# Layer 1's cross-attention in a decoder kernel: from two rounds over all queries to four quarters, with two key tiles in TensorE's row halves and the next quarter's maxima beside the units

## The chip, the cores and the metric

The kernel runs on one core of a Trainium2 chip. The metric is the device time of one execution in microseconds, lower is better. Of the engines, PE is TensorE, DVE is VectorE, ACT is ScalarE, POOL is GpSimd and SP is SyncE; each runs its own instruction stream and waits on semaphores. PE's clock has two levels, 1.2 and 2.4 GHz; the profile gives the granted share of the higher one.

## The reference

The kernel computes a two-layer decoder on x (1,024 tokens of 128 features) with a context of 6,404 rows of 96 features. What matters here is layer 1's cross-attention. Keys and values come from the context by two quantized projections to `image_embeds`, and the queries are `fused` (1,024 × 128):

```python
for Wa, ba in ((W_att0, b_att0), (W_att1, b_att1)):
    kv = bitnet_linear(image_embeds, Wa, ba)          # 6404 x 64
    k = jnp.concatenate([kv, kv], axis=-1)
    scores = jnp.einsum('bse,bpe->bsp', fused, k) * inv_sqrt_e
    attn = jax.nn.softmax(scores, axis=-1)
    fused = fused + 0.1 * jnp.einsum('bsp,bpe->bse', attn, k)
```

It is two rounds of softmax attention, the second on the first one's result. As the keys are the same 64 features twice, the kernel adds the two halves of `fused` once and works with 64 features. Both uses of `kv`, as keys and as values, go through the same attention.

## The kernel before

**Tiles.** The 6,404 keys are 51 tiles of 128 (KT, the last with 4 keys); 26 units (NU) hold two tiles each, the last one tile. Scores stand in PSUM with keys on partitions and queries along the row. Queries are split into halves of 512 (HALF).

**A round** (r = 0, 1) has a head and a loop.

The head: PE multiplies `fused` by DUP (L2044), ACT copies the queries to f16 (L947, QH) and DVE makes the low part (L1499, QL). Then `max_alone` finds, for each query, the maximum over all keys. It uses max(a, b) = (a + b)/2 + |a − b|/2: PE makes half-differences (bank 0 or 2 and the one behind) and half-sums (bank 4 or 6 and the one behind) from LK16 (L1692), ACT writes the magnitudes (L717, MC), and DVE adds and reduces both in one instruction (L1078). ALONE1 lists its steps: 3 chunks of 1,024 times 8 query tiles, and a rest of 130 columns for all tiles, so 24 large evictions and 8 small ones on DVE. `shifts` (L1099) and `diagonals` (L1105) turn the maxima into diagonal matrices, and `seeds` (L1714) puts −maximum into the four score banks.

The loop over 26 units: `scores` (L1729) accumulates three products of high and low f16 parts per tile (KL·QH, KH·QL, KH·QH); in each, two matmuls with 64 rows, one per query half, use the two row halves of PE and write banks 2b and 2b+1. ACT takes exp of a tile for all 1,024 queries (L738) into PR, two units deep. PE multiplies it with the values of the tile in fp32 (L1744), behind the scores of the next unit; the two query halves go to the two column halves. DVE adds each tile to ACC (L1128). At the end, `denominators` (L1756) sums ACC over partitions, DVE takes reciprocals (L1134) in two halves and normalizes (L1143), adds the bias (L1517) and updates `fused` in XT (L1521); `fused_upd` lets PE go on with round 1's head.

**Work beside.** In round 0's loop the keys and values of round 1 are prepared: 14 SIDES (sums and differences for the maxima, L1906 and L1907, evicted by ACT at L861 and L864) in bank 5, and 20 NEXT_KV: 7 groups of values (L1898, L847) and 13 of keys (L1892 and L1893, high part by ACT at L841, low part by DVE at L1439) in banks 6 and 7. Round 1's loop has nothing beside it.

**Layer 0** has a cross-attention of the same form. There the maxima of the next pair of heads run beside the loop: `max_steps` on PE (L1776), `magnitude` on ACT (L758), `maximum` on DVE (L1078), 512 columns a step, with bank 6 for the one half and bank 7 for the other. A step waits for two counters, and DVE's loop sets where its part stands:

```python
e.wait_ge(S("x_cp"), micro_base(p) + m)        # max_steps, PE
e.wait_ge(S("mx"), micro_base(p) + m - 1)

add_up(*before, 0)                              # loop, DVE
maximum(p, first)
add_up(*before, 1)
maximum(p, last)
```

**Order.** Each engine's order is written out by hand in the loops over units; nothing is planned at run time. The next stage (f1, f2 and the low-rank tail) waits for the maximum of the updated `fused` (L1524 to L1526), which POOL reduces over partitions (L608). SP loads that stage's weights (L493, L494) once the last unit's buffers are free.

Of the kernel before, what the change touches and what calls it, by code (L numbers as in the profile page):

```python
# [69 lines left out]
ALONE1 = full_then_rest(NDC - 1, lambda t: (t % 2,), 6)  # L70
# [16 lines left out]
def unit_no(hf, i):  # L87
    return hf * NU + i
# [104 lines left out]
def kv_bank(x):  # L193
    return 6 + NEXT_KV.index(x) % 2


def kv_freed(r, x):

    if x[0] == "dk":
        return "lk_lo", r * NKP + x[1] + 1  # L200
    return "vt_ev", r * NVT + x[1] + 1

# [35 lines left out]
def build_decoder(nc, x_tm, x_fm, ctx_fm, small, pair_w, moe_w, sh_gu, sh_d, bit_w, lr_a, lr_b, out):  # L238
    with ExitStack() as ctx:
# [33 lines left out]
        TMPB = KN[1][:, 4 * T:4 * T + 2 * LAG].bitcast(F32)  # L273
# [123 lines left out]
        AVG = sb("AVG", [P, 4])  # L397
# [21 lines left out]
        OO = W_[1]  # L419
# [8 lines left out]
        def attention_operands(hf):  # L428

            if hf < 2 * PAIRS:  # L430
                p, u = divmod(hf, 2)
                q = [slice(u * HALF, (u + 1) * HALF)] * 2
                kh, kl, qh, ql = KH, KL, QH[p % 2], QL[p % 2]
                shift = [DIAG[:, h, 4 * u:4 * u + 4, :].rearrange("p a b -> p (a b)") for h in range(2)]

                def v(r, j, h):
                    return V[0:r, j, h * HD:(h + 1) * HD]
            else:
                n = hf - 2 * PAIRS
                q = [slice(h * HALF, (h + 1) * HALF) for h in range(2)]  # L440
                kh, kl, qh, ql = LKH[n], LKL[n], QH[1], QL[1]
                shift = [DIAG[:, h, 0:4, :].rearrange("p a b -> p (a b)") for h in range(2)]

                def v(r, j, h):
                    return V2[n][0:r, j, :]
            return kh, kl, qh, ql, q, shift, v
# [5 lines left out]
        def _(q):  # L452
# [38 lines left out]
            q.wait_ge(S("pv"), unit_no(2 * PAIRS + 1, NU - 1) + 1)  # L491
            q.wait_ge(S("acc"), (2 * PAIRS + 2) * KT)
# [11 lines left out]
        def _(e):  # L504
# [87 lines left out]
            e.sem_inc(S("dup"), 1)  # L592
            e.wait_ge(S("ln_x"), 2 * NT)
# [12 lines left out]
            for i in range(3, 6):  # L606
                e.wait_ge(S("ax"), i + 1)
# [8 lines left out]
        def _(e):  # L616
# [327 lines left out]
            for r in range(2):  # L944
# [1228 lines left out]
```

## Time and profile before

| | |
|---|---|
| runs | 1724.82, 1729.21 (median), 1729.83 us |
| profiled execution | 1728.0 us, span 1726.3 us, mean granted clock 0.916 |
| PE busy | 1516.9 us (88%) |
| DVE busy | 1291.2 us (75%) |
| ACT busy | 1118.8 us (65%) |
| POOL busy | 433.0 us (25%) |
| chain that ended last | PE 64%, DVE 14%, issue 13%, POOL 5%, ACT 3% |

Busy shares are averages over stages with different limits, so they only say where to look first. The chain is followed back from the last instruction, at each step to what released it; "issue" is time in which an engine waited for nothing that the profile shows. A matmul's recorded duration holds its way through the array, so where matmuls follow each other, the distance from start to start is what each costs.

### The profile page before, as it was taken

The numbers are of one execution on the slowest core, as the hardware profiler recorded it, in microseconds if no ns is written. First come the engines' busy times: TensorE is split into PE (matmuls) and PEld (weight loads), VectorE is DVE, ScalarE is ACT, GpSimd is POOL, SyncE is SP. The second block draws the span as 40 slices with busy tenths as digits, with TensorE's granted clock in tenths as the row PEclk, the third lists the DMA queues.
The fourth block names the chain that finished last, engine by engine and source line by source line (L and its number), as shares of the span: only waits on it lengthen the run. The fifth ranks groups of instructions, "written<-read, shape, count | busy, mean of one in ns | idle before, by whom it ended". The sixth has DMA issues, their size and how long they took to land.

```text
span 1726.3 us, 26028 instructions
## 1 busy us (share of the span) xinstructions
PE 1516.9 (88%) x8864; PEld 542.1 (31%) x8864; DVE 1291.2 (75%) x2214; ACT 1118.8 (65%) x1496; POOL 433.0 (25%) x413
## 2 busy tenths in 40 slices
PE   3878889999999999999999997899996869978963
PEld 2412223333333333333332333343333612311312
DVE  4798688777888778887789898766665676778775
ACT  3687667776777767867767686655553466746633
POOL 5401333343443434433400010344441000000000
PEclk7966889999999999999999998999998958986986
DMA  4000000000000000000010000111100000000000
GB/s 127 7 0 6 1 1 2 1 1 1 8 1 1 1 1 3 1 1 10 20 32 1 1 1 22 32 41 46 41 27 0 1 0 1 1 1 1 1 13 12
DMA packets 12556, 20.26 MB, mean 12 GB/s; under 512 B 1670, under 2 KB 11254, under 8 KB 12342
## 3 DMA queue, kind: packets, MB, share of 16 engines
q1 hardware_dynamic: 12438, 18.76, 3.9%
q8 instruction: 66, 1.08, 0.3%
q14 instruction: 52, 0.43, 0.1%
HBM read 18.23 MB, written 0.52 MB: 11 GB/s over the span
## 4 chain that ended last, share of the span: by engine, by line
PE 64%; DVE 14%; issue 13%; POOL 5%; ACT 3%; DMA 1%; POOLq 0%; SPq 0%; ACTq 0%; DVEq 0%
PE PS L1744 26%; PE PS L1729 18%; PE PS L1776 4%; POOL WRK L599 4%; DVE KNB L1078 4%; PE PS L1692 3%; PE PS L1619 2%; PE PS L1611 2%; DVE WRK L1128 1%; DMA KNB<-in_ctx_fm_dram 1%; DVE QS L1134 1%; PE PS L2020 1%; PE PS L2005 1%; ACT KNB L758 1%; ACT WRK L738 1%
## 5 line engine op out<-in xcount | busy, mean ns | idle before, releaser
L1128 DVE TENSOR_TENSOR WRK<-WRK 128x768 f32<-128x768 f32 (+1 forms) x500 | 550.4, 1101 | 57.2 <-ACT WRK L738 45.1
L738 ACT ACTIVATE WRK<-PS 128x1024 f32<-128x1024 f32 (+1 forms) x510 | 500.0, 1022 | 104.9 <-PE PS L1729 90.7
L1744 PE MATMUL PS<-WRK,V 128*64 128x512 f32 (+1 forms) x2040 | 498.0, 608 | 0.0
L1078 DVE CUSTOM_DVE_ANT_0 KNB<-PS,KNB 128x512 f16<-128x512 f32 (+2 forms) x464 | 331.4, 731 | 150.9 <-PE PS L1776 139.0
L572 POOL TENSOR_TENSOR WRK<-WRK 128x256 f32<-128x256 f32 x300 | 277.8, 926 | 411.7 <-ACT WRK L738 394.5
L758 ACT ACTIVATE KNB<-PS 128x512 f16<-128x512 f32 (+2 forms) x306 | 181.1, 592 | 108.3 <-PE PS L1776 108.2
L1916 PE MATMUL PS<-WRK,KNB 128*128 128x512 f16 x828 | 198.1, 384 | 11.0 <-POOL WRK L599 4.3
L1744 PEld LDWEIGHTS PS<-WRK,V 128*64 128x64 f32 (+1 forms) x2040 | 124.3, 136 | 247.8 <-issue 199.1
L1729 PE MATMUL PS<-Q,KB 64*128 64x512 f16 (+1 forms) x1428 | 192.7, 379 | 0.5 <-ACT WRK L738 0.4
L1729 PE MATMUL PS<-KNB,KB 64*128 64x512 f16 (+1 forms) x1224 | 156.3, 377 | 0.0
L599 POOL TENSOR_TENSOR WRK<-KB,WRK 128x1024 f16<-128x1024 f32 x46 | 98.6, 2143 | 133.9 <-ACT WRK L884 133.9
L1916 PEld LDWEIGHTS PS<-WRK,KNB 128*128 128x128 f16 x828 | 77.3, 98 | 123.1 <-issue 23.1
L717 ACT ACTIVATE KNB<-PS 128x1024 f16<-128x1024 f32 x96 | 97.9, 1023 | 27.3 <-DVE MXP L1078 15.5
L1300 DVE TENSOR_TENSOR KA<-PS,KB 128x1024 f32<-128x1024 f32 x46 | 56.3, 1224 | 72.6 <-ACT KB L871 72.6
L884 ACT ACTIVATE WRK<-KB 128x1024 f16<-128x1024 f32 x46 | 48.6, 1057 | 90.3 <-DVE KB L1306 87.0
L1729 PEld LDWEIGHTS PS<-Q,KB 64*128 64x128 f16 (+1 forms) x1428 | 65.5, 94 | 128.8 <-ACT WRK L738 44.1
L1776 PE MATMUL PS<-KNB,Q 64*128 64x512 f16 (+1 forms) x448 | 80.0, 360 | 27.5 <-DVE MXP L1078 17.0
L608 POOL PARTITION_ALL_REDUCE AM<-AX x3 | 1.1, 371 | 380.6 <-DVE AX L1526 295.6
L1729 PEld LDWEIGHTS PS<-KNB,KB 64*128 64x128 f16 (+1 forms) x1224 | 59.9, 94 | 63.5 <-issue 12.0
L1692 PE MATMUL PS<-CTX,Q 64*128 64x512 f16 x192 | 50.8, 606 | 15.0 <-DVE MXP L1078 7.0
L1729 PE MATMUL PS<-Q,KA 64*128 64x512 f16 (+1 forms) x408 | 62.0, 383 | 0.0
L666 ACT ACTIVATE V<-PS 128x512 f32<-128x512 f32 (+1 forms) x52 | 30.1, 580 | 48.6 <-PE PS L1619 48.0
(333 smaller groups left out, 1501.0 us busy)
## 6 DMA issues: line engine op xcount, KB each, us to landing
V<-in_moe_w_dram SPq DMA_DIRECT2D x44, 192.0 KB, 2.4
KNB<-in_ctx_fm_dram SPq DMA_DIRECT2D x1, 2401.5 KB, 18.5
CTX<-in_ctx_fm_dram SPq DMA_DIRECT2D x6, 384.0 KB, 4.4
BW<-in_bit_w_dram SPq DMA_DIRECT2D x1, 960.0 KB, 6.2
PWK<-in_pair_w_dram SPq DMA_DIRECT2D x4, 192.0 KB, 2.6
SM<-in_small_dram SPq DMA_DIRECT2D x1, 716.5 KB, 4.6
XT<-in_x_fm_dram SPq DMA_DIRECT2D x1, 512.0 KB, 5.5
X<-in_x_tm_dram SPq DMA_DIRECT2D x1, 512.0 KB, 7.4
```

What stands on the lines that cost most here:

```text
L572: e.tensor_tensor(total, total, part, ALU.add).then_inc(S("acc_pool"), 1)
L599: e.tensor_tensor(H_LO[hslot], MH[hslot % 2], H_HI[hslot], ALU.subtract).then_inc(S("h_lo"), 1)
L717: e.activation(MC[:, m % 2, :], bank(b, b + 2), ACT.Abs).then_inc(S("x_cp"), 1)
L738: e.activation(PR[0:r, u % 2, b, :], bank(2 * b, 2 * b + 2, slice(0, r)), ACT.Exp).then_inc(S("exp"), 1)
L758: e.activation(MC[:, m % 2, 0:w], PS[:, 6, 0:w], ACT.Abs).then_inc(S("x_cp"), 1)
L1078: return e.tensor_tensor_reduce(diffs, sums, diffs, 0.5, NEG, ALU.add, ALU.max, accum_out=out)
L1128: e.tensor_tensor(total, total, part, ALU.add).then_inc(S("acc"), 1)
L1692: ins = e.matmul(o, queries[rows, tiles[0] * P:(tiles[0] + 1) * P], keys[rows, at:at + HALF], start=True, stop=True)
L1729: ins = e.matmul(PS[0:r, 2 * b + h, :], keys[rows, j * P:j * P + r], queries[rows, q[h]], start=False, stop=(k == 2), skip_group_check=True)
L1744: ins = e.matmul(PS[h * HD:(h + 1) * HD, 4, :], v(r, j, h), PR[0:r, unit_no(hf, i) % 2, b, h * HALF:(h + 1) * HALF], start=(j == 0), stop= ...
L1776: ins = e.matmul(PS[:, b, k * w:(k + 1) * w], QH[(p + 1) % 2][rows, t * P:(t + 1) * P], K16[rows, off + a:off + a + w], start=True, stop=True)
L1916: ins = e.matmul(bank(b + h), w_[:, part, :], rows[:, h * HALF:(h + 1) * HALF], start=start and i == 0, stop=stop and i == 2, skip_group_c ...
```

## The change

Instead of two rounds over 1,024 queries there are four quarters n: round n // 2, query half n % 2. A quarter has 26 units of two key tiles and 512 queries. In `scores1` the two row halves of PE hold the two tiles of a unit; in `values1` the two column halves sum even and odd tiles apart, and a matmul with DUP (`fold`) adds the halves at the end. Only quarter 0's maxima run alone, for half of the queries; those of quarter n + 1 run in quarter n (STEPS1, 26 steps of 512 columns or a rest), from unit 0 in quarter 0 and from unit 8 in quarters 1 and 2. The exponentials have four buffers (PR1). Keys and values of round 1 are spread over quarter 0 (14 sides, 7 values, 5 keys) and quarter 1 (8 keys), all in bank 5. The queries of quarters 2 and 3 are projected in unit 6 of quarters 1 and 2, after `fold` has updated their half of `fused` in unit 4. POOL adds the bias to XT ahead of time. The distance of the key differences is 512 instead of 256, and the quantization of the queries (L1491) loses its clamps.

Constants and lists:

```diff
-ALONE1 = full_then_rest(NDC - 1, lambda t: (t % 2,), 6)
+ALONE1 = [(d, [t], t % 2) for d in range(NDC - 1) for t in range(NT // 2)] + [(NDC - 1, [0, 1, 2, 3], 0)]
...
+STEPS1 = [(c, [t], t % 2) for c in range(NFULL) for t in range(NT // 2)] + [(NFULL, [0, 1, 2], 0), (NFULL, [3], 1)]
+NM1 = len(STEPS1)
...
+def steps1(n, i):
...
+    first, last = (0 if n == 0 else 8), NU - 2
+    if n + 1 == QUARTERS or not first <= i <= last:
+        return []
+    k = last - first + 1
+    return list(range((i - first) * (NM1 + 1) // k, (i - first + 1) * (NM1 + 1) // k))
...
+def items1_of(n):
+    at = {i: [] for i in range(NU)}
+    if n == 0:
+        for k, x in enumerate(SIDES):
+            at[k].append(("side", x))
+        for k, x in enumerate(NEXT_KV[:NU - len(SIDES)]):
+            at[len(SIDES) + k].append(x)
+    else:
+        at[1].append(("den", n - 1))
+        at[2].append(("den2", n - 1))
+        at[4].append(("fold", n - 1))
+        if n < 3:
+            at[6].append(("query", n + 1))
+        if n == 1:
+            for k, x in enumerate(NEXT_KV[NU - len(SIDES):]):
+                at[0 if k == 0 else 7 + k].append(x)
+    return at
```

POOL:

```diff
+                if i == 4:
+                    for k, (r, part) in enumerate(((0, slice(0, T)), (1, slice(0, HALF)), (1, slice(HALF, T)))):
+                        e.wait_ge(S("f2_ps"), k + 1)
+                        e.tensor_scalar(XT[:, part], XT[:, part], BT1[:, r:r + 1], None, ALU.add).then_inc(S("pre_b"), 1)
```

ACT:

```diff
+            def exp1(n, i):
...
+                e.wait_ge(S("sc"), BEFORE_SC + t + 1)
+                if t >= len(PR1):
+                    e.wait_ge(S("pv"), BEFORE_PV + t - len(PR1) + 1)
+                    e.wait_ge(S("acc"), BEFORE_SC + t - len(PR1) + 1)
...
+                    ins = e.activation(PR1[t % len(PR1)], bank(b, b + 2), ACT.Exp)
...
+            def magnitude1(n, steps):
...
+                    e.wait_ge(S("x_ps"), k + 1)
+                    e.wait_ge(S("mx"), k - 1)
+                    e.activation(MC[:, (k - BASE1) % 2, 0:w], PS[:, 6, 0:w], ACT.Abs).then_inc(S("x_cp"), 1)
...
+            for n in range(QUARTERS):
                 for i in range(NU):
...
+                    magnitude1(n, steps1(n, i)[0:1])
+                    exp1(n, i)
+                    magnitude1(n, steps1(n, i)[1:])
+                    if i == 0 and n:
+                        copy_out1(n - 1)
+                    for x in ITEMS1[n][i]:
+                        bank5_1(x)
```

DVE:

```diff
-            quantize(XQ, bank(0, 2), XF, 3).then_inc(S("quant"), 1)
+            link(e.tensor_scalar(XF, bank(0, 2), AI[:, 3:4], MAGIC, ALU.mult, ALU.add))
+            e.tensor_scalar(XQ, XF, MAGIC, None, ALU.subtract).then_inc(S("quant"), 1)
...
+            def maximum1(n, steps):
...
+                for s in steps:
+                    m = s - 1
...
+                    e.wait_ge(S("y_ps"), k + 1)
+                    e.wait_ge(S("x_cp"), k + 1)
+                    for z, t in enumerate(tiles):
+                        ins = half_max(MXP[:, 4 * ((n + 1) % 2) + t, c:c + 1], PS[:, 7, z * w:(z + 1) * w],
+                                       MC[:, (k - BASE1) % 2, z * w:(z + 1) * w])
+                    ins.then_inc(S("mx"), 1)
...
+            def fold(n):
...
+                e.scalar_tensor_tensor(XT[:, part], bank(5), 0.1, XT[:, part], ALU.mult,
+                                       ALU.add).then_inc(S("fused_upd"), 1)
...
+            for quarter in range(QUARTERS):
                 for i in range(NU):
...
+                    if i:
+                        add_up1(quarter, i - 1)
+                    elif quarter:
+                        add_up1(quarter - 1, NU - 1)
+                    maximum1(quarter, steps1(quarter, i))
+                    for x in ITEMS1[quarter][i]:
+                        bank5_1(x)
+                    if quarter + 1 < QUARTERS and i == NU - 1:
+                        shifts1(quarter + 1)
```

PE:

```diff
+            def scores1(n, i):
...
+                if t >= 2:
+                    e.wait_ge(S("exp"), BEFORE_SC + t - 1)
+                if i < 2:
+                    e.wait_ge(S("diag"), 2 * PAIRS + n + 1)
+                    for g in range(2):
+                        e.matmul(bank(b + g), ones16[:, :], DIAG[:, u, 0:4, :].rearrange("p a b -> p (a b)"), start=True,
+                                 stop=False, skip_group_check=True)
+                for k, (keys, queries) in enumerate(((LKL[r], QH[1]), (LKH[r], QL[1]), (LKH[r], QH[1]))):
+                    for g in tiles_of(i):
+                        j = 2 * i + g
+                        w = rows_of(j)
+                        rows = slice(g * HD, (g + 1) * HD)
+                        ins = e.matmul(PS[0:w, b + g, :], keys[rows, j * P:j * P + w], queries[rows, q], start=False,
+                                       stop=(k == 2), skip_group_check=True)
...
+            def values1(n, i):
...
+                e.wait_ge(S("exp"), BEFORE_SC + t + 1)
...
+                for g in tiles_of(i):
+                    j = 2 * i + g
+                    w = rows_of(j)
+                    ins = e.matmul(PS[g * HD:(g + 1) * HD, 4, :], V2[n // 2][0:w, j, :],
+                                   PR1[t % len(PR1)][0:w, g * HALF:(g + 1) * HALF], start=(i == 0),
+                                   stop=(j >= KT - 2), skip_group_check=True)
...
+            def denominators1(n):
+
+                e.wait_ge(S("acc"), BEFORE_SC + (n + 1) * NU)
+                for k in range(2):
+                    for g in range(2):
+                        ins = e.matmul(PS[g * HD:(g + 1) * HD, 5, :], ones[:, 0:HD],
+                                       ACC[:, n % 2, k * HALF:(k + 1) * HALF], start=(k == 0), stop=(k == 1),
...
+            def fold(n):
+
+                e.wait_ge(S("on"), 2 * PAIRS + n + 1)
+                e.matmul(bank(5), DUP, ON[:, n % 2 * HALF:(n % 2 + 1) * HALF], start=True,
...
+            def max_steps1(n, steps):
...
+                    if m < NM1:
+                        e.wait_ge(S("x_cp"), base + m)
+                    e.wait_ge(S("mx"), base + m - 1)
+                    if m < NM1:
+                        max_half1(n, m, 0, 6, "x_ps")
+                    if m:
+                        max_half1(n, m - 1, NH, 7, "y_ps")
...
                 for i in range(NU):
...
+                    max_steps1(n + 1, steps1(n, i)[0:1])
+                    scores1(n, i)
+                    max_steps1(n + 1, steps1(n, i)[1:])
+                    for x in ITEMS1[n][i]:
+                        bank5_1(x)
                     if i:
...
+                        values1(n, i - 1)
+                    elif n:
+                        values1(n - 1, NU - 1)
+            values1(QUARTERS - 1, NU - 1)
+            denominators1(QUARTERS - 1)
+            fold(QUARTERS - 1)
```

## Rows read from the trace of the kernel before

**Rows 1.** Busy time by stage: start:end, length, busy time by engine, PEclk, DMA share, GB/s

```profile
1394.27:1429.64 35.37, 26.95 (x112) 5.21 (x112) 31.80 (x67) 27.00 (x28) 0.00 (x0) 0.50 0.00 1
1429.64:1531.12 101.48, 101.48 (x621) 30.65 (x621) 71.84 (x66) 70.71 (x87) 0.00 (x0) 0.98 0.00 1
1531.12:1582.60 51.48, 32.84 (x126) 6.90 (x124) 40.32 (x77) 27.34 (x29) 0.00 (x0) 0.58 0.00 1
1582.60:1667.55 84.95, 84.46 (x511) 25.18 (x510) 61.97 (x51) 49.55 (x51) 0.00 (x0) 0.99 0.00 1
```

**Rows 2.** Timeline, head of round 0: start, us, engine, line, operation [idle before <-releaser]

```profile
1384.14 0.69 DVE L1230 TENSOR_SCALAR WRK<-WRK 128x1024 f32<-128x1024 f32 x1
...
1396.49 1.23 DVE L1078 CUSTOM_DVE_ANT_0 KNB<-PS,KNB 128x1024 f16<-128x1024 f32 x1 [2.36 <-ACT KNB L717]
...
1428.29 1.29 DVE L1105 TENSOR_TENSOR DIAG<-ident,NEGM 128x512 f16<-128x512 f16 x2
1429.64 1.89 PE L1714 MATMUL PS<-DIAG,ones 128*128 128x512 f16 x4 [2.91 <-DVE DIAG L1105]
```

**Rows 3.** Timeline, one unit of round 1

```profile
1657.41 0.39 PE L1729 MATMUL PS<-Q,KB 64*128 64x512 f16 x2
...
1658.27 1.94 ACT L738 ACTIVATE WRK<-PS 128x1024 f32<-128x1024 f32 x2 [1.33 <-PE PS L1729]
...
1658.81 1.94 PE L1744 MATMUL PS<-WRK,V 128*64 128x512 f32 x8
...
1659.33 2.56 DVE L1128 TENSOR_TENSOR WRK<-WRK 128x1024 f32<-128x1024 f32 x2 [0.71 <-ACT WRK L738]
...
1660.67 0.39 PE L1729 MATMUL PS<-Q,KB 64*128 64x512 f16 x2
```

**Rows 4.** Timeline: one tile's scores (round 1's end), one tile's values (layer 0)

```profile
1663.94 0.38 PE L1729 MATMUL PS<-Q,KB 64*4 64x512 f16 x2
...
1664.68 0.65 PE L1744 MATMUL PS<-WRK,V 128*64 128x512 f32 x2
...
1043.54 1.03 PE L1744 MATMUL PS<-WRK,V 128*64 128x512 f32 x4
...
1044.50 1.47 PE L1729 MATMUL PS<-Q,KB 64*128 64x512 f16 x12
```

**Rows 5.** Timeline of layer 0: a maxima pair, then two pairs in a one-tile unit

```profile
483.91 0.39 PE L1776 MATMUL PS<-KNB 64*128 64x512 f16 x2
484.13 1.46 PE L1729 MATMUL PS<-Q,KB 64*128 64x512 f16 x12
...
277.65 0.39 PE L1776 MATMUL PS<-KNB,Q 64*128 64x512 f16 x2
...
278.11 0.69 DVE L1078 CUSTOM_DVE_ANT_0 KNB<-PS,KNB 128x512 f16<-128x512 f32 x1 [0.44 <-PE PS L1776]
...
278.95 0.39 PE L1776 MATMUL PS<-KNB,Q 64*128 64x512 f16 x2 [0.17 <-DVE MXP L1078]
```

**Rows 6.** Timeline of layer 0: PE held by a late maximum on DVE

```profile
226.61 0.68 DVE L1078 CUSTOM_DVE_ANT_0 KNB<-PS,KNB 128x512 f16<-128x512 f32 x1
...
227.22 0.95 DVE L1128 TENSOR_TENSOR WRK<-WRK 128x768 f32<-128x768 f32 x1
...
227.45 0.61 PE L1776 MATMUL PS<-KNB,Q 64*128 64x512 f16 x2 [7.29 <-DVE MXP L1078]
```

**Rows 7.** Groups by form, 1428.6 to 1534.4: count | busy us, mean ns | idle before

```profile
L738 ACT ACTIVATE WRK<-PS 128x1024 f32<-128x1024 f32 x50 | 48.6, 1024 | 8.6 <-PE PS L1729 7.8
...
L1439 DVE SCALAR_TENSOR_TENSOR KB<-PS,WS,KA 128x512 f16<-128x512 f32 x11 | 8.3, 751 | 1.4 <-ACT KA L841 1.3
...
L841 ACT ACTIVATE KA<-PS,WS 128x512 f16<-128x512 f32 x11 | 7.6, 687 | 11.9 <-PE PS L1893 11.9
```

**Rows 8.** Timeline of the tail

```profile
1672.81 1.97 DVE L1517 TENSOR_SCALAR WRK<-ON,SM 64x512 f32<-64x512 f32 x4
...
1677.92 0.35 POOL L608 PARTITION_ALL_REDUCE AM<-AX  x1 [295.58 <-DVE AX L1526]
```

More of the change, by code:

```diff
@@ L592, in _ @@
             e.sem_inc(S("dup"), 1)
+            for r in range(2):
+                link(e.tensor_scalar(BT1[:, r:r + 1], sm(f"b_att{r}"), 0.1, None, ALU.mult))
             e.wait_ge(S("ln_x"), 2 * NT)
@@ new lines, in bank5_1 @@
+            def bank5_1(x):
+                kind, a = x
+                if kind == "side":
+                    sums_and_differences(1, *a, 5)
+                elif kind == "query":
+                    part = slice(a % 2 * HALF, (a % 2 + 1) * HALF)
+                    e.wait_ge(S("f2_ps"), a)
+                    if a == 2:
+                        e.wait_ge(S("sc"), BEFORE_SC + NU)
+                    else:
+                        e.wait_ge(S("sc"), BEFORE_SC + 2 * NU)
+                    e.activation(QH[1][:, part], bank(5), ACT.Copy, scale=D ** -0.5).then_inc(S("f2"), 1)
+                elif kind in ("values", "dk"):
+                    kv(1, x)
@@ new lines, in max_half1 @@
+            def max_half1(n, m, off, b, name):
+                c, tiles, g = STEPS1[m]
+                r, u = divmod(n, 2)
+                a, w = MCH[c]
+                rows = slice(g * HD, (g + 1) * HD)
+                for k, t in enumerate(tiles):
+                    ins = e.matmul(PS[:, b, k * w:(k + 1) * w], QH[1][rows, (4 * u + t) * P:(4 * u + t + 1) * P],
+                                   LK16[r][rows, off + a:off + a + w], start=True, stop=True)
+                ins.then_inc(S(name), 1)
@@ new lines, in _, with bank5_1 @@
+            order1 = {x: k for k, x in enumerate(ORDER1)}
+            def bank5_1(x):
+                kind, a = x
+                if kind == "den2":
+                    return
+                if order1[x]:
+                    name, count = freed1(ORDER1[order1[x] - 1])
+                    e.wait_ge(S(name), count)
+                if kind == "side":
+                    sums_and_differences(1, *a, 5, 0)
+                elif kind == "den":
+                    denominators1(a)
+                elif kind == "fold":
+                    fold(a)
+                elif kind == "query":
+                    e.wait_ge(S("fused_upd"), a - 1)
+                    e.matmul(bank(5), DUP, XT[:, a % 2 * HALF:(a % 2 + 1) * HALF], start=True,
+                             stop=True).then_inc(S("f2_ps"), 1)
+                else:
+                    kv(1, x)
```

299 lines of the change are left out of this document (178 added, 121 removed).

## The prediction

> **What bounds the kernel now.** I read the page first: PE is busy for 88% of the span and holds 64% of the chain that ended last, so PE is the suspect. An average doesn't tell what one stage is worth, so I cut layer 1's cross-attention into its stages [rows 1]. Both unit loops are PE's: 101.48 and 84.95 us in which PE is busy throughout at a granted clock of 0.98 and 0.99. The head of a round is not: in the 35.37 us before the first loop DVE is busy for 31.80, and PE's clock is at 0.50, its lower level (1.2 GHz). Between the loops 51.48 us go by with the same head and the end of round 0. So there are some 87 us in which PE could do other work, and that is what the change is after.
>
> In a unit of round 1 [rows 3] the score matmuls start at 1657.41, exp at 1658.27 (0.86 later), the value matmuls at 1658.81, and the next unit at 1660.67: 3.26 us for two key tiles and all 1,024 queries. The two row halves already work at the same time: two matmuls together are recorded as 0.39 long, and twelve start within 1.40 us.
>
> **The change, part by part.** The sum is made against the profiled execution's 1728.0 us, which is 1.2 below the median of the runs.
>
> *Head.* Between DVE's first large eviction and the diagonals [rows 2] lie 24 large and 8 small evictions, 31.8 us. The new list has 12 and 4: −15.9. One diagonal of two: −0.65. Two shift matmuls of four ahead of the first scores: −0.9. The quantization drops one pass of 0.69. Together −18.1.
>
> *Packing.* Two key tiles in the row halves instead of two query halves saves no PE time: six matmuls per tile and 1,024 queries before, six per two tiles and 512 queries after. It makes the units smaller: 104 instead of 52. With one tile's scores between, values start 0.74 after scores (three passes of 0.22 and 0.09 of change-over), and one tile's values take 0.96 until the next scores [rows 4]: 1.70 a unit, where half of 3.26 is 1.63. So 104 units cost 7 us more than 52 did. The Trainium skill (TensorEngine Tiling (Array Packing), Key Properties) states that a change of tiling mode drains TensorE, and scores and values use different modes; the trace agrees in direction, 0.07 a unit. Without it the sum would be 7 lower.
>
> *Other PE work.* A pair of maxima matmuls, sums and differences in opposite row halves, holds PE for 0.22 [rows 5]; 27 steps a quarter make 5.9 in each of quarters 0 to 2. Round 0's loop is longer than round 1's by 16.5; less 1.9 for its four shifts at low clock, 14.6 is the price of its 34 side, value and key items: 0.43 each. Denominators take two fp32 passes instead of one, 1.85 (twice 0.93, half of the 1.86 of [rows 3]); a fold and a query projection 0.95 each, at the same price; shifts for two units 1.0.
>
> PE alone would need: quarter 0: 44.2 + 5.9 + 26 × 0.43 + 0.5 − 0.96 (no values in its first unit) = 60.8; quarter 1: 44.2 + 5.9 + 8 × 0.43 + 1.0 + 1.85 + 1.9 = 58.4; quarter 2: 54.9; quarter 3: 48.0. Sum 222.1, with 1.0 for the last values 223.1.
>
> *The new wait.* Maxima have one bank for sums (6) and one for differences (7). In quarters 1 and 2 they may run in units 8 to 24 alone: 27 steps in 17 units, so 10 units hold two. There PE issues step a, scores, step b, then the value matmuls; step b waits until DVE has evicted the differences that step a issued. Nothing on PE passes that wait: values, and the next unit's scores, stand behind it. In layer 0 this round trip shows: a at 277.65, eviction at 278.11, b at 278.95 with "<-DVE MXP" [rows 5]: 1.30, where PE alone would need 0.87. And there DVE was free. When DVE is late, PE's wait is as long as that takes: 7.29 us once [rows 6], from an eviction's start to PE 0.84.
>
> Here DVE is late in each such unit, since it first adds up the unit before: 1.23 [rows 3], of which the next instruction overlaps 0.05. From the start of that addition, b comes 1.18 + 0.84 = 2.02 later; the differences that b issues reach DVE 0.46 later [rows 5], their eviction takes 0.62 (226.61 to 227.22) [rows 6], and the next addition can start: 3.10 a unit, after another such unit. After a unit with one step the addition itself waits for exp: 0.22 (pair) + 0.86 + 1.02 + 0.04 = 2.14 [rows 3, 5, 7] after that unit's start, which is 0.22 into the next; b at 2.24, then 0.22 + 0.09 + 0.96 [rows 4]: 3.51. PE alone would need 1.70 + 0.44 = 2.14. A unit with one step stays at 1.92: its wait ends 1.81 after its start. So a pair of steps costs 0.96 or 1.37 of pure waiting.
>
> Quarter 2 has 7 of the one kind and 3 of the other: 12.5. Quarter 1 has 6 without key items (4 × 1.37 + 2 × 0.96 = 7.4, and 0.7 where the two kinds meet), and 4 with one: there ACT evicts the key item behind the second magnitude, DVE takes another 0.75 behind ACT's 0.69 [rows 7], and the next addition waits for that. The same count gives 4.8 after one single and 4.4 after another double, where PE needs 2.6: 3 × 2.1 + 1.8 = 8.1.
>
> Smaller waits: the fold behind 3.4 us of reciprocals, 0.6 in each of quarters 1 to 3; the shifts at the ends of quarters 1 and 2, 0.6 each; in quarter 0 two double units 3.0, bank 5's key items handed on through DVE 2.0, the low clock of its first units 1.3, its end, where the shifts stand behind a key item on DVE, 2.0.
>
> Quarters: 60.8 + 8.3 = 69.1; 58.4 + 17.4 = 75.8; 54.9 + 13.7 = 68.6; 48.0 + 0.6 = 48.6. With the last values 263. Before, from the first scores to the denominators, 236.1 (1431.5 to 1667.55) [rows 1]. So +26.9: the 51.5 between the loops are gone, and the loops themselves take 78 more.
>
> *Tail.* Denominators +0.9. From 1672.81 to the all-reduce at 1677.92 [rows 8], 5.1, is replaced by a fold at low clock (two passes of 0.85 and 0.25 of hand-over), an addition over half the width (0.7 and a gap of 0.2), half a maximum (0.6) and 0.25: 3.85. Net −0.35.
>
> *At nothing.* POOL's three additions of the bias: POOL is idle in all four stages [rows 1], and each is wanted tens of us later. ACT needs 2.2 us of a 2.4 us unit in quarter 0; if it doesn't fit, up to 0.2 in 14 units, 3 us, which the range holds. SP's last loads stand behind the same event as before, and their consumers behind the fold. No DMA is added.
>
> Sum: −18.1 + 26.9 − 0.35 = +8.4 on 1728.0; on the median, **1738**.
>
> **Rivals.**
> *Faster: the second step costs its round trip alone.* If DVE has its addition behind it when step a issues, each of the 20 double units waits 0.43 [rows 5] instead of 0.96 to 2.1: 8.6 instead of 28.0, so 11.0 below before: 1718. For it: in layer 0 two steps a slot cost PE nothing but their 0.22 when scores of two tiles lay between. Against: there an eviction stands ahead of the addition on DVE, here the addition stands ahead in the code, and it can't start before exp is done. It decides where the mean wait of a double unit is under 1.0 us. If nothing waited at all, 223 us of PE time would give 1698.
> *Slower: PE's clock falls.* In the double units PE streams for some 60 to 70% of the time. In the head its clock is 0.50 with evictions as the pace [rows 1]; in both loops, with PE busy throughout, 0.98 or more. No row shows a stage between these. At the lower level each unit takes 1.7 longer; for half of the 34 units with maxima +29: 1766. The Trainium skill (TensorE: Matmul & The Clock Gate, Part 1) states that this clock is gated by how busy PE has been; the trace agrees, with 0.50 in the head.
> *It doesn't do what it says: maxima don't run beside.* If the first step of a quarter waited for the query projection of its unit 6, steps would bunch up. The projection is done about 3.4 us after unit 6 starts, two units take longer than that; I give it nothing.
>
> **How the numbers follow.** 0.65 for the forecast, 0.20 for the round trip alone, 0.05 for no waits, 0.10 for the clock. The forecast's own range is 1727 to 1751: a third of its 40 us of waits either way. The range that holds 8 in 10, 1712 to 1752, adds the first rival; 1698 and 1766 stay out. A measurement of this kernel tells 0.3%, 5 us, from no change. Forecast: 0.42 slower, 0.18 within, 0.05 faster; round trip: 0.16 faster, 0.04 within; no waits: faster; clock: slower. Together 0.26 faster, 0.22 same, 0.52 slower.
>
> **What would show it.** Right: the head some 16 us shorter; quarters of about 69, 76, 68 and 49 us; in quarters 1 and 2, units 8 to 24, PE idle before the second maxima pair with DVE's maxima as releaser, about 1 to 2 us each, and DVE's addition right before that eviction; units of 1.70 in quarter 3. Wrong: quarters 1 and 2 at 60 or less, idle time under 0.5 before those pairs (first rival); a granted clock under 0.9 in quarter 1 or 2 (second); units of quarter 3 far from 1.70 (packing mis-sized).

## The result, and the profile after

The kernel after takes 1742.36 us in the median of its runs (1741.44 to 1742.88) against 1727.03 for the kernel before, measured beside it (four runs, three of them those of the table ahead, whose median is 1729.21): a ratio of 1.0087, 95% interval 1.0073 to 1.0101. That is 15 us slower. The profiled execution took 1741.99, its span 1740.3.

The first view is the busy time in windows, one for each quarter from its first shift matmul to the next quarter's (the last one to the denominators), then four windows around the end of quarter 0. The columns are those of [rows 1].

```profile
1412.51:1485.26 72.75, 67.94 (x398) 18.04 (x401) 50.72 (x90) 56.66 (x79) 0.00 (x0) 0.92 0.00 1
1485.26:1562.66 77.40, 63.59 (x341) 16.17 (x344) 57.43 (x98) 47.13 (x62) 1.56 (x1) 0.98 0.00 1
1562.66:1630.76 68.10, 58.13 (x329) 15.06 (x328) 52.04 (x90) 42.46 (x54) 1.56 (x1) 1.00 0.00 1
1630.76:1681.74 50.98, 50.70 (x273) 11.87 (x271) 36.47 (x34) 26.76 (x27) 0.00 (x0) 1.00 0.00 1
...
1469.00:1477.00 8.00, 5.73 (x38) 1.73 (x34) 7.43 (x11) 5.61 (x9) 0.00 (x0) 1.00 0.00 0
1478.47:1485.26 6.79, 5.90 (x13) 0.96 (x14) 3.56 (x6) 1.96 (x3) 0.00 (x0) 0.50 0.00 0
1485.26:1488.71 3.45, 3.45 (x11) 0.67 (x12) 0.45 (x1) 1.00 (x1) 0.00 (x0) 0.50 0.03 7
1488.71:1493.00 4.29, 3.53 (x16) 0.90 (x18) 1.35 (x2) 2.23 (x4) 0.00 (x0) 1.00 0.00 0
```

Where [rows 1] had both loops filled by PE, PE now stands for 4.8, 13.8 and 10.0 us of quarters 0 to 2; only the last quarter, which has no maxima beside it, is PE's throughout. Around the end of quarter 0, from 1478.47 to 1488.71, the granted clock is 0.50, the lower level (1.2 GHz).

The waits of PE from 1409 to 1690 us, by line and releaser (total us, times, longest), name the cause in their first row: L2283 is the matmul of a maxima step. The second row is the folds; its longest wait, 4.2, is that of the tail.

```profile
PE PS L2283 <- DVE MXP L1193: 25.5, 24, 1.8
PE PS L2273 <- DVE ON L1258: 5.0, 4, 4.2
PE PS L2235 <- DVE DIAG L1617: 1.7, 2, 1.1
```

The timeline of the kernel after (start, us, engine, line, operation, idle time before and its releaser), in four pieces: the head's first maxima matmul and the first shift matmul behind it; the end of quarter 0; a unit of quarter 2 with two steps; a unit of quarter 3, and the tail.

```profile
1393.62 1.86 PE L1871 MATMUL PS<-CTX,Q 64*128 64x512 f16 x6 [2.54 <-DVE Q L1607]
...
1412.51 1.04 PE L2235 MATMUL PS<-DIAG,ones 128*128 128x512 f16 x2 [1.11 <-DVE DIAG L1617]
...
1477.79 0.23 PE L2283 MATMUL PS<-CTX,Q 64*128 64x130 f16 x1 [1.78 <-DVE MXP L1193]
...
1478.49 1.97 PE L2255 MATMUL PS<-WRK,V 128*64 128x512 f32 x4
...
1480.39 0.58 PE L2242 MATMUL PS<-Q,KB 64*4 64x512 f16 x1
...
1489.62 0.60 PE L2235 MATMUL PS<-DIAG,ones 128*128 128x512 f16 x2
...
1589.41 0.39 PE L2283 MATMUL PS<-CTX,Q 64*128 64x512 f16 x2
...
1589.57 1.23 DVE L1632 TENSOR_TENSOR WRK<-WRK 128x1024 f32<-128x1024 f32 x1 [0.58 <-ACT WRK L1020]
...
1590.71 0.68 DVE L1193 CUSTOM_DVE_ANT_0 KNB<-PS,KNB 128x512 f16<-128x512 f32 x1
...
1591.55 0.39 PE L2283 MATMUL PS<-CTX,Q 64*128 64x512 f16 x2 [1.10 <-DVE MXP L1193]
...
1591.87 1.08 PE L2255 MATMUL PS<-WRK,V 128*64 128x512 f32 x4
...
1592.88 0.39 PE L2283 MATMUL PS<-CTX,Q 64*128 64x512 f16 x2
...
1647.27 0.39 PE L2242 MATMUL PS<-Q,KB 64*128 64x512 f16 x2
...
1648.02 1.08 PE L2255 MATMUL PS<-WRK,V 128*64 128x512 f32 x4
1649.03 0.39 PE L2242 MATMUL PS<-Q,KB 64*128 64x512 f16 x2
...
1681.74 1.94 PE L2265 MATMUL PS<-WRK,ones 128*64 128x512 f32 x8
...
1687.88 2.08 PE L2273 MATMUL PS<-ON,DUP 128*128 128x512 f32 x2 [4.20 <-DVE ON L1258]
...
1691.73 0.38 POOL L670 PARTITION_ALL_REDUCE AM<-AX  x1 [110.80 <-DVE AX L1705]
```

The head, from its first maxima matmul at 1393.62 to the first shift matmul at 1412.51, is 18.9 us long, where [rows 1] had 35.37. In the double unit the first step is issued at 1589.41. Its half-sums lie ready, but DVE adds up the preceding unit's weights until 1590.71, then evicts them, and the second step starts at 1591.55; the values follow it. The unit takes 3.47 us, of which PE stands for 1.10. A plain unit of quarter 3 takes 1.76 us, 0.75 from scores to values and 1.01 from values to the next scores. From the denominators at 1681.74 to the all-reduce are 9.99 us, 10.37 before (1667.55 to 1677.92 in [rows 1, 8]).

So the head and the tail are shorter, and still the all-reduce comes at 1691.73 instead of 1677.92 [rows 8], 13.8 us later. The time went into the quarters.

### The profile page after: what moved, and what is told of

The parts are those of the page before. It is cut to its first block, busy times and chain, and to the rows that moved or that the text cites. A ratio compares the mean times of both kernels' runs of the same rounds, so it can differ in the third digit from the quotient of the medians.

```text
span 1740.3 us, 26359 instructions
## 1 busy us (share of the span) xinstructions
PE 1528.2 (88%) x8887; PEld 538.7 (31%) x8900; DVE 1293.7 (74%) x2290; ACT 1131.2 (65%) x1537; POOL 442.5 (25%) x418
## 4 chain that ended last, share of the span: by engine, by line
PE 62%; DVE 14%; issue 14%; POOL 5%; ACT 4%; DMA 1%; POOLq 0%; DVEq 0%; SPq 0%; ACTq 0%
PE PS L1922 20%; PE PS L1908 13%; PE PS L2255 5%; PE PS L1954 4%; POOL WRK L657 4%; DVE KNB L1193 4%; PE PS L2242 3%; PE PS L1798 2%; PE PS L1790 2%; PE PS L1871 2%; PE PS L2283 1%; DVE WRK L1243 1%; DVE QS L1249 1%; DMA KNB<-in_ctx_fm_dram 1%; PE PS L2196 1%
## 5 line engine op out<-in xcount | busy, mean ns | idle before, releaser
L800 ACT ACTIVATE WRK<-PS 128x1024 f32<-128x1024 f32 (+1 forms) x408 | 400.9, 1022 | 58.2 <-PE PS L1908 44.5
L1243 DVE TENSOR_TENSOR WRK<-WRK 128x768 f32<-128x768 f32 (+3 forms) x400 | 427.2, 1068 | 14.2 <-ACT WRK L800 7.6
L1922 PE MATMUL PS<-WRK,V 128*64 128x512 f32 (+1 forms) x1632 | 398.9, 609 | 0.0
L1922 PEld LDWEIGHTS PS<-WRK,V 128*64 128x64 f32 (+1 forms) x1632 | 99.7, 136 | 197.0 <-issue 161.9
L1908 PE MATMUL PS<-Q,KB 64*128 64x512 f16 (+1 forms) x1224 | 152.6, 377 | 0.0
L1632 DVE TENSOR_TENSOR WRK<-WRK 128x1024 f32<-128x1024 f32 (+1 forms) x100 | 119.9, 1199 | 29.5 <-ACT WRK L1020 28.4
L1020 ACT ACTIVATE WRK<-PS 128x1024 f32<-128x1024 f32 x100 | 102.4, 1024 | 53.6 <-PE PS L2242 50.2
L2255 PE MATMUL PS<-WRK,V 128*64 128x512 f32 (+1 forms) x408 | 113.8, 626 | 0.3 <-issue 0.3
L1410 DVE TENSOR_TENSOR KA<-PS,KB 128x1024 f32<-128x1024 f32 x46 | 56.3, 1225 | 72.7 <-ACT KB L934 72.7
L1908 PEld LDWEIGHTS PS<-Q,KB 64*128 64x128 f16 (+1 forms) x1224 | 55.6, 94 | 89.1 <-ACT WRK L800 21.1
L779 ACT ACTIVATE KNB<-PS 128x1024 f16<-128x1024 f32 x60 | 61.2, 1024 | 17.4 <-DVE MXP L1193 9.7
L1044 ACT ACTIVATE KNB<-PS 128x512 f16<-128x512 f32 (+1 forms) x78 | 45.3, 581 | 32.5 <-PE PS L2283 31.9
```

The lines of the kernel that those rows point to most:

```text
L800: e.activation(PR[0:r, u % 2, b, :], bank(2 * b, 2 * b + 2, slice(0, r)), ACT.Exp).then_inc(S("exp"), 1)
L1243: e.tensor_tensor(total, total, part, ALU.add).then_inc(S("acc"), 1)
L1632: e.tensor_tensor(total, total, part, ALU.add).then_inc(S("acc"), 1)
L1908: ins = e.matmul(PS[0:r, 2 * b + h, :], keys[rows, j * P:j * P + r], queries[rows, :], start=False, stop=(k == 2), skip_group_check=True)
L1922: ins = e.matmul(PS[h * HD:(h + 1) * HD, 4, :], V[0:r, j, h * HD:(h + 1) * HD], PR[0:r, unit_no(hf, i) % 2, b, h * HALF:(h + 1) * HALF], s ...
L2255: ins = e.matmul(PS[g * HD:(g + 1) * HD, 4, :], V2[n // 2][0:w, j, :], PR1[t % len(PR1)][0:w, g * HALF:(g + 1) * HALF], start=(i == 0), st ...
```

## The experiments

Theory W says that PE stands because the reduction of a unit's first step waits on DVE behind the addition, and the second step, the values and the next unit wait for it. Theory M says that the halved units cost, since PE goes from scores (64 rows) to values (128 rows) and back twice as often. Theory C says that the low clock at the end of quarter 0 carries the loss.

The code ahead of the first shift matmul is the same in all these kernels, yet in their profiles that matmul starts anywhere between 1409.29 and 1417.26 us. So I compare one stretch by the traces, from that matmul to the all-reduce of the tail, and give the time beside it. Quarters 0 to 2 run from their first shift matmul to the next quarter's.

One part of this stretch comes from no edit. From the denominators to the all-reduce most of these kernels take 9.99 us, but e4, e6 and e10 take 9.04 (e11 9.82). What differs is the fold of the tail, 2.08 us in after at the lower clock, and in e6:

```profile
1665.49 1.12 PE L2301 MATMUL PS<-ON,DUP 128*128 128x512 f32 x2 [4.20 <-DVE ON L1284]
```

So 0.95 us are taken off below where the stretch of e4, e6 or e10 is compared.

| kernel | quarters 0, 1, 2 | stretch | time against before (95%) |
|---|---|---|---|
| after | 72.75, 77.40, 68.10 | 279.22 | 1.0087 (1.0073 to 1.0101) |
| e1 reduction first | 69.00, 69.75, 65.16 | 264.87 | 1.0004 (0.9993 to 1.0014) |
| e2 values in twos | 71.66, 83.46, 75.06 | 288.80 | 1.0117 (1.0100 to 1.0134) |
| e3 both | 70.56, 75.54, 67.11 | 271.83 | 1.0044 (1.0027 to 1.0061) |
| e4 no maxima beside | 62.67, 57.29, 51.61 | 231.58 | 1692.17 us, one run |
| e5 e1, twos in quarter 3 | 68.99, 69.73, 65.15 | 262.21 | 0.9970 (0.9959 to 0.9981) |
| e6 e1, GpSimd adds | 68.99, 67.82, 62.27 | 258.81 | 0.9956 (0.9939 to 0.9973) |
| e7 e1, shifts first | 68.11, 69.27, 64.69 | 263.04 | 0.9974 (0.9964 to 0.9985) |
| e8 e1, e5, e6, e7 | 67.50, 67.58, 62.03 | 255.19 | 0.9930 (0.9914 to 0.9946) |
| e9 e1 in quarter 0 alone | 68.99, 76.98, 68.10 | 275.04 | 1734.88 us, one run |
| e10 e1 in quarters 1, 2 | 72.74, 71.28, 65.15 | 269.17 | 1729.29 us, one run |
| e11 shorter addition | 69.99, 75.00, 65.29 | 270.80 | 1729.15 us, one run |

### e1: the reduction ahead of the addition

```
+                    maximum1(quarter, steps1(quarter, i)[0:1])
                     if i:
                         add_up1(quarter, i - 1)
...
-                    maximum1(quarter, steps1(quarter, i))
+                    maximum1(quarter, steps1(quarter, i)[1:])
```

> Edit: on DVE the first maxima reduction of a unit runs ahead of the addition of the preceding unit's weights, the second behind it (after has both behind it). Theory W (PE stands because the first reduction waits behind the 1.23 us addition: 25.5 us in 24 waits in after's trace): the waits of the second step fall from 1.10-1.80 us to under 0.3, a double unit of quarter 2 goes from 3.47 and 3.04 us to about 2.8, one with a key item from 4.7 to about 3.6, and the time falls by 12 to 20 us, to 1722-1730. Rival M (each unit is dear because TensorE changes between products of 64 and of 128 rows twice a unit): the plain unit of the last quarter stays at 1.76 us, the wait only moves to the next unit's first step, and the time falls by 4 us at most. Rival C (the half clock at the end of quarter 0 carries the loss): a gain only if the stall before it, 5.73 us busy in 8, goes: up to 5 us.

The time fell by 15.5 us to 1726.84, the stretch by 14.35. In e1's timeline a double unit of quarter 2 reads thus:

```profile
1575.35 0.39 PE L2284 MATMUL PS<-CTX,Q 64*128 64x512 f16 x2
...
1575.81 0.69 DVE L1193 CUSTOM_DVE_ANT_0 KNB<-PS,KNB 128x512 f16<-128x512 f32 x1 [0.16 <-PE PS L2284]
...
1576.42 1.22 DVE L1632 TENSOR_TENSOR WRK<-WRK 128x1024 f32<-128x1024 f32 x1
...
1576.65 0.39 PE L2284 MATMUL PS<-CTX,Q 64*128 64x512 f16 x2 [0.27 <-DVE MXP L1193]
...
1578.40 0.39 PE L2284 MATMUL PS<-CTX,Q 64*128 64x512 f16 x2 [0.35 <-DVE MXP L1193]
```

The eviction now starts 0.46 after the step, and the second step waits 0.27 instead of 1.10 (0.67 in a unit with a key item, where under 0.3 had been expected). Counted as in after, from a unit's first step to the next unit's, a double unit takes 3.05 us, behind a single or a double one alike, and 3.57 with a key item; a single one stays at 1.98. PE's waits for this releaser in e1:

```profile
PE PS L2284 <- DVE MXP L1193: 12.7, 37, 0.7
```

They halved in sum, but there are 13 more of them: the second reduction now stands behind the addition, and the next unit's first step waits for it (0.35 in the last line above), so that a double unit takes 3.05 and not the 2.8 expected. A single and a double unit together went from 5.45 to 5.03. W held. The plain unit stayed at 1.76, and part of the wait moved to the next unit's first step, both as M had it, but the gain is far above the 4 us that M allowed.

### e2 and e3: the values of two units together

```
-                    if i:
-                        values1(n, i - 1)
...
+                    t = turn(n, i)
+                    if t % 2 and t >= 3:
+                        for v in (t - 3, t - 2):
+                            values1(v // NU, v % NU)
```

(ACT copies a quarter's values out one unit later.) e3 has e1's order as well.

> Edit: the values of two units are multiplied together after the scores of two units, so that PE passes from 64-row to 128-row products once in two units where it did in each; DVE's order is after's. W: the double units stand as long as before, so only the plain units move, if at all: 0 to -6 us (1736-1742). M: a plain unit falls from 1.76 us to 1.63-1.70, -6 to -13 us over 104 units (1729-1736), with the same waits for the reductions. C: no change.

> Both edits together. W with a small M: the gains add, -18 to -27 us, 1715-1724, below the 1727 of the kernel before. M alone: -6 to -13. If the second reduction is late for the next unit's first step, the gains do not add: about 1728.

Both came out the other way: e2's stretch is 9.58 longer than after's, e3's 6.96 longer than e1's. e2's time, 1748.22 us, is outside all that had been expected. e3's, 1734.81, lies where M alone had been put, but it has that from e1's order, less what the twos cost. Two plain units did fall to 3.27 us in quarter 3, as M had it. But where maxima run, the waits grew. In e2's waits:

```profile
PE PS L2283 <- DVE MXP L1193: 30.9, 31, 2.8
PE PS L2283 <- ACT KNB L1044: 4.9, 6, 1.0
```

With the values of two units put together, the steps of the two units come closer to each other, and DVE and ACT don't keep up. At the end of quarter 2 two units with three steps took 6.31 us, 5.45 in after (3.47 + 1.98); earlier in it, where the double unit is the first of the two, 5.48. That the values between the steps had given the reductions time fits this, but no run tests it by itself. In e2 the clock takes part too: five times in quarters 1 and 2 it was at its lower level for 3.4 us (0.50 from 1508.1 to 1511.5, the first of them), and PE was busy nearly throughout. In e3 that happened once (from 1540.4 to 1543.8), so there it can't be the whole loss, and the waits for DVE's maxima are 23.3 us, 12.7 in e1.

### e4: the maxima beside the quarters left out

This kernel leaves out the maxima of quarters 1 to 3 and makes their shifts from those of quarter 0.

```
-    if n + 1 == QUARTERS or not first <= i <= last:
+    if True:
         return []
...
-                e.wait_ge(S("mx"), base1(n) + (NM1 if n else len(ALONE1)))
+                e.wait_ge(S("mx"), BASE1 + len(ALONE1))
...
```

> Leaves out the maxima of quarters 1 to 3 (their shifts are made from quarter 0's maxima); all else is after's. W: 78 steps of 0.44 us of PE (34 us) and the waits for them (30 us) go: about 1680, each quarter 26 units of 1.76 us and its items, 46 to 50 us, quarter 0 with its side and key items 55 to 60. M: the plain unit stays at 1.76 us everywhere. C: the clock still falls at the end of quarter 0, since the key items pass one bank one after another: quarter 0 over 62 us.

The time was 1692.17, the stretch 231.58, or 232.53 with after's tail. So the maxima beside the quarters cost 46.7 us in after and 32.3 in e1. The expected 1680 had a step at 0.44 us of PE. It is 0.22 for its two matmuls, which lie in opposite row halves: a unit of quarter 0 with a side item takes 2.26 us here and 2.47 in after. 78 steps are then 17 us of PE, and some 30 of the 46.7 are waits and the low clock, 15 of the 32.3. With 0.22 the same sum gives 1742 − 17 − 30 = 1695. Quarter 0 took 62.67 us, where 55 to 60 had been expected and over 62 was C's sign, but the clock does not fall at its end. The two longest units near its end, with a key item each, take 3.65 and 3.82 us, as in e1.

### e5: values in twos where no maxima run

```
+                    if n == 3 and 2 <= i < NU - 1 and i % 2 == 0:
+                        continue
+                    for v in range(t - (2 if n == 3 and i >= 3 and i % 2 else 1), t):
+                        if v >= 0:
+                            values1(v // NU, v % NU)
```

> Edit: e1's order of reductions, and in the last quarter, which has no maxima beside it, the values of two units together. M by itself (a passage from scores to values and back costs PE 0.25 us: 3.27 us for two units in the last quarter of e2, 3.52 in e1): 11 pairs, -2.8 us against e1, 1723-1725. If the cost of the passage were hidden, as after e1 the additions on DVE could be the bound: no change from e1's 1726.8.

The stretch is 2.66 shorter than e1's. In e5's timeline of quarter 3 two units are 3.27 apart:

```profile
1652.16 0.39 PE L2243 MATMUL PS<-Q,KB 64*128 64x512 f16 x2
...
1653.56 1.94 PE L2256 MATMUL PS<-WRK,V 128*64 128x512 f32 x8
1655.43 0.39 PE L2243 MATMUL PS<-Q,KB 64*128 64x512 f16 x2
```

That is the 3.26 of [rows 3], where after has 3.52: one passage from scores to values and back costs 0.25 us.

### e6 and e11: GpSimd takes a quarter of each addition

```
-                r, w = (P, T) if len(tiles_of(i)) > 1 else (TAIL, HALF)
+                r, w = (P, SHARE) if len(tiles_of(i)) > 1 else (TAIL, HALF)
...
+                part = PR1[t % len(PR1)][:, SHARE:T]
+                total = ACC[:, n % 2, SHARE:T]
+                    e.tensor_tensor(total, total, part, ALU.add).then_inc(S("acc_pool"), 1)
```

The lower two lines and their waits are new on GpSimd; SHARE is 768. e6 has this with e1's order, e11 with after's.

> Edit: e1's order, and GpSimd adds 256 of the 1024 columns of each unit's weights, as it does in layer 0, so that DVE's addition is 0.95 us in place of 1.23. W to its end (what PE still stands in e1, 12.1 us in 36 waits, is DVE's load: 3 reductions and 2 additions, 4.8 us, in the 5.03 us of two units): two units of quarter 2 fall from 5.03 to 4.84, with a key item from 6.09 to about 5.6, and the time falls by 4 to 7 us against e1, to 1720-1723. Rival: the waits are round trips (reduction ends, PE's next step 0.2-0.4 us later) and stay: within 2 us of e1, and GpSimd's adds of 0.73 us slow DVE's.

> Edit: after's order, but GpSimd takes 256 of the 1024 columns of each addition, so that DVE's is 0.95 us in place of 1.23. W (the second step waits for the rest of the addition ahead of its reduction): each double unit is shorter by what the addition is shorter, 3.47 us to 3.2, and the 25.5 us of waits fall by about 0.28 us each, by 6 to 8 us in all with quarter 0's end. Rival (the wait is the round trip of the reduction alone, whatever stands ahead of it): the doubles stay at 3.47.

e11's stretch is 8.42 shorter than after's. Its double unit in the timeline:

```profile
1580.68 0.39 PE L2310 MATMUL PS<-CTX,Q 64*128 64x512 f16 x2
1580.84 0.96 DVE L1658 TENSOR_TENSOR WRK<-WRK 128x768 f32<-128x768 f32 x1 [0.85 <-ACT WRK L1046]
1580.89 1.50 POOL L679 TENSOR_TENSOR WRK<-WRK 128x256 f32<-128x256 f32 x1 [2.56 <-ACT WRK L1046]
...
1581.72 0.69 DVE L1219 CUSTOM_DVE_ANT_0 KNB<-PS,KNB 128x512 f16<-128x512 f32 x1
...
1582.56 0.39 PE L2310 MATMUL PS<-CTX,Q 64*128 64x512 f16 x2 [0.84 <-DVE MXP L1219]
```

The addition is 0.27 shorter, PE's wait 0.26, the double unit 0.26 (3.21). The wait is the rest of the addition, and a round trip behind it: from the eviction's start to the step 0.84, as in after (1590.71 to 1591.55). e6's stretch is 6.06 shorter than e1's, 5.11 without the tail: two units of quarter 2 take 4.77 us where e1 had 5.03. PE alone would need 4.18 (two of 1.76 and three steps of 0.22), so 0.6 of waits is left; the 4.84 of the expectation had the step at 0.44. Units with a key item stayed at 3.57; there I had expected a gain.

### e7 and e8: shifts ahead of the addition, and all together

```
                     maximum1(quarter, steps1(quarter, i)[0:1])
+                    if quarter + 1 < QUARTERS and i == NU - 1:
+                        shifts1(quarter + 1)
                     if i:
                         add_up1(quarter, i - 1)
...
-                    if quarter + 1 < QUARTERS and i == NU - 1:
-                        shifts1(quarter + 1)
```

> Edit: e1's order, and in the last unit of a quarter the next quarter's shifts are made ahead of the addition of the preceding unit. Each of the three quarter starts waits 0.41 us for the shifts in e1; that goes: -1.2 us against e1, 1725.6, too little to be told in the time, but plain in the trace (the seeds' wait at the three starts).

> e1, e5, e6 and e7 together. If the gains add: -8 to -11 us against e1, 1716-1719, 0.5% below the kernel before. If e6 gives nothing: 1723.

e7's stretch is 1.83 shorter than e1's (1.2 expected), and PE waits for the shifts at the start of the first quarter alone. The waits that went were 1.46, 0.41 and 0.41 in e1, not three of 0.41. The stretch gives back less than their sum, for the second unit of quarter 0 took 4.29 us and in e1 3.64; there the clock was still at 0.50 in e7. e8's is 9.68 shorter than e1's, where the three gains add to 9.60 (without the 0.95 of e6's tail): they about add. At 0.9930 of the kernel before (1717.42 us), e8 is faster than the kernel before and the one after. Its quarters in windows:

```profile
1413.14:1480.64 67.50, 65.53 (x400) 17.69 (x400) 43.57 (x89) 56.47 (x79) 22.06 (x26) 0.97 0.00 1
1480.64:1548.22 67.58, 62.65 (x345) 16.22 (x344) 52.40 (x98) 46.44 (x62) 20.72 (x26) 1.00 0.00 1
1548.22:1610.25 62.03, 58.77 (x330) 15.55 (x328) 47.02 (x90) 41.46 (x54) 21.46 (x26) 1.00 0.01 1
```

PE now stands for 2.0, 4.9 and 3.3 us of them.

### e9 and e10: the new order in quarter 0 alone, and in the others alone

```
+                    k = 1 if quarter == 0 else 0
+                    maximum1(quarter, steps1(quarter, i)[0:k])
                     if i:
                         add_up1(quarter, i - 1)
...
-                    maximum1(quarter, steps1(quarter, i))
+                    maximum1(quarter, steps1(quarter, i)[k:])
```

e10 has `quarter > 0` there.

> Edit: e1's order in quarter 0 alone, after's order in quarters 1 and 2. C (the fall of TensorE's clock at the end of quarter 0 comes from PE standing behind that quarter's last reductions): the clock stays at 1.00 in the 24 us around the end of quarter 0, quarter 0 takes 69.0 us as in e1 (after 72.75), quarter 1 about 75.5 (after 77.4, its start no longer at the low clock), quarter 2 68.1 as in after: -5 to -6 us from the first shifts in the score banks to the all-reduce. Rival: the clock falls anyway, since the key items stay: quarter 0 over 71 us.

> Edit: the complement of e9: e1's order in quarters 1 and 2, after's in quarter 0. W: quarter 0 72.75 us with the low clock at its end, quarter 1 about 71.5 (e1's 69.75 and what the low clock takes from its start), quarter 2 65.2: -8 to -9 us on the same stretch. Rival (what was won in e1 hangs on quarter 0): under -4.

e9's stretch is 4.18 shorter than after's, e10's 10.05, or 9.10 without the tail. Together that is 13.28, where e1 has 14.35. In e9 the clock no longer falls at the end of quarter 0, though the key items are there; nor does it in e11 (1.00 from 1471.0 to 1482.2), which has after's order and shorter additions. Both edits shorten the longest wait of the last steps behind the additions (1.78 us in after, 0.65 in e9, 1.51 in e11), so the fall at this place hangs on those waits. Clock and waits together are 3.76 us of quarter 0. Quarter 1 took 76.98 where I had expected 75.5: there the clock fell later, in e9's windows

```profile
1470.00:1478.28 8.28, 6.01 (x31) 1.58 (x32) 7.44 (x18) 4.50 (x7) 0.00 (x0) 1.00 0.00 0
1500.00:1505.00 5.00, 3.06 (x17) 0.77 (x18) 3.08 (x6) 3.51 (x5) 0.00 (x0) 1.00 0.00 0
1505.00:1510.00 5.00, 5.00 (x20) 0.99 (x18) 2.94 (x6) 3.20 (x5) 0.00 (x0) 0.66 0.00 0
```

behind the wait of its first double unit with a key item, and so it did in e11. In after three such units, with waits of 1.80 each, left it at 1.00, so which waits bring it down is not settled here. In e10 the low clock after quarter 0 costs quarter 1 1.53 us (71.28 against e1's 69.75).

What the clock costs without the waits for maxima shows in the last unit of quarter 0 and the first of quarter 1, which hold no step. In after they run from 1480.39 to 1485.26 and on to 1489.62, 4.87 and 4.36 us. In e9 they take 3.82 and 2.81 (in e11 3.81 and 2.81):

```profile
1474.46 0.37 PE L2244 MATMUL PS<-Q,KB 64*4 64x512 f16 x1
...
1478.28 0.59 PE L2237 MATMUL PS<-DIAG,ones 128*128 128x512 f16 x2 [1.46 <-DVE DIAG L1617]
...
1481.09 0.60 PE L2237 MATMUL PS<-DIAG,ones 128*128 128x512 f16 x2
```

So C is true of 2.6 us in these two units, and of 5.3 at most (3.76 and 1.53) with the waits ahead of them: a part of the loss, not the most of it.

## Why the prediction was right, step by step

The forecast was slower by 8.4 us on the profiled execution; the all-reduce came 13.8 later, and the median is 15 above. The mechanism was the forecast's, some sizes were off.

- *Head, −18.1.* First shift matmul 18.9 us after the first maxima matmul, then one shift pair instead of two: first scores at 1413.48, before at 1431.47: −18.0. From the head's first maxima matmul on it is −17.3, where the forecast without the quantization's 0.69 has −17.4. That 0.69 lies ahead of it, where traces of the same code differ by several us, so the last 0.6 of the agreement is luck.
- *The new wait.* Forecast: 3.51 for a double unit after a single, 3.10 after a double, 1.92 for a single, 4.8 with a key item. Measured: 3.47, 3.04, 1.98 and 4.71. A double unit without a wait would be 2.20 (1.76 and two steps of 0.22) and not 2.14, so PE stood for 1.27 and 0.84 of it, where 1.37 and 0.96 had been forecast. It was forecast that DVE's addition stands right ahead of the eviction; e1 takes it away from there and e11 shortens it, and the wait follows both. (The prediction has the two banks the wrong way round: in the code bank 6 takes the half-differences, for ACT, and bank 7 the half-sums, which DVE evicts. The wait is the same.) Quarter 2 from its first scores to the next quarter's: forecast 68.6, measured 68.1; quarter 1: 75.8 and 77.0.
- *Quarter 0, the step that failed.* Forecast 69.1, measured 72.7 from scores to scores. The forecast had given its end 2.0 us for shifts behind a key item and no clock. It priced the clock as a rival with its place in the units of quarters 1 and 2, where it is 0.98 and 1.00; in its real place, the end of quarter 0 and the start of quarter 1, it was at the lower level for 10.2 us. There it took 2.6 us of two units without a step, and with the waits ahead of them 5.3 (3.76 in quarter 0, after against e9, and 1.53 in quarter 1, e10 against e1). The units with a side item are another part: 2.47 us, where the forecast's 1.70, 0.22 and 0.43 make 2.35, some 1.3 us in eleven of them.
- *The sum.* From first scores to denominators 268.3 us, forecast 263. Against the forecast quarter 0 is 3.6 longer, quarter 1 1.2, quarter 3 with the last values 0.8, and quarter 2 is 0.5 shorter: 5.1 of the 5.4 between +8.4 and +13.8. Two slips in the prediction's arithmetic change nothing: quarter 1's PE time adds to 58.3, not 58.4, and a third of 40 us below 1738 is 1725, not 1727.
- *Packing, mis-sized.* The plain unit was to be 1.70 and is 1.76, since one tile's values take 1.01 until the next scores and not 0.96: I had taken that from a unit of layer 0 [rows 4]. Halving the units costs 0.13 a unit (e5), not 0.07. The Trainium skill (TensorEngine Tiling (Array Packing), Key Properties) states that a change of tiling mode drains TensorE; e5, which halves the changes and returns to 3.27 for two units, agrees. In quarter 3, which is PE's alone, it shows: 50.4 from the first scores to the denominators instead of 49.6.
- *Tail, −0.35.* Measured −0.38, with the fold at the lower clock, as forecast; with the tail of e6, e4 or e10 it would have been −1.33.
- *First rival, the round trip alone, 1718.* e1 is that case, made by hand, and it comes out at 1726.8, level with before. The rival's price had left out that a reduction put ahead of the addition leaves the other one behind it: 12.7 us of waits stay, 0.2 to 0.4 us each in the units of quarter 2. With those shortened (e6), values in twos where nothing else needs the gaps (e5) and the shifts first (e7), it is 1717 (e8).

The change's account, from the first maxima matmul of the head to the all-reduce: before 283.65 us (1394.27 to 1677.92 in [rows 1, 8]), after 298.11, 14.5 more. With e4's stretch, at after's tail, behind after's head it is 251.4: without the maxima beside, the change would be 32.2 us below before. The head's 16.5 is half of that; the other half is not taken apart here, but round 1's own maxima, which are gone from between the loops, lie in it. The maxima beside then cost 46.7, of which 17 is PE's work and 30 is waits and clock. Swapping two instructions on DVE gives 14.4 of it back (e1), which makes it level; e8 gives back 24.0.

## What to carry to other kernels

Work that runs beside a loop is bought at the price of the waits it puts on the loop's engine: follow each new wait to the instruction that ends it, and look at what stands ahead of that one in its own queue. Swapping two instructions on an engine that was not the bottleneck gave back 14 us here. Count how often a smaller unit changes between kinds of matmul, and group them only where nothing else needs the gaps.

## What was not expected

- In after the granted clock fell to its lower level at the end of quarter 0, behind 8 us in which PE was busy for 5.73 and no wait of PE was longer than 1.78 us; in e9 it fell behind 5 us with 3.06 busy. The rest of quarter 1 and all of quarter 2 of after, with PE standing for 10 us and more, kept 1.00. When it falls, the values of a unit go from 1.08 to 1.97 us.
- Until the first shift matmul the traces of kernels with the same code up to there differ by up to 8.0 us, while quarters behind it agree to 0.02 us from kernel to kernel (quarter 0: 69.00, 68.99, 68.99, 68.99 in e1, e5, e6, e9). The head, too, is 18.89 us long in all of them but e7 (18.49), and the tail's fold has two lengths. A difference of a few us in the time of one run says less than a stretch of its trace, and a stretch less than one whose clock has been looked at.
- In e11 the addition that begins second, GpSimd's or DVE's, takes longer. GpSimd's 256 columns took 1.50 us behind DVE's start, in the lines of e11 above, and 0.73 ahead of it, in the lines below. DVE's 768 columns took 0.96 in most units, little over three quarters of its 1.23 for 1,024, and up to 1.48 where GpSimd had begun:

```profile
1591.26 0.73 POOL L679 TENSOR_TENSOR WRK<-WRK 128x256 f32<-128x256 f32 x1 [2.48 <-ACT WRK L1046]
...
1591.57 1.23 DVE L1658 TENSOR_TENSOR WRK<-WRK 128x768 f32<-128x768 f32 x1
```

Spans on GpSimd are rough.
